# Who makes the low rows' one-hots of the input products of steps 0 and 1: ScalarE in place of GpSimd

## What is computed

```
def cell(h, x):                              # 64 steps, in order
    gi = x @ W_ih + b_ih
    gh = h @ W_hh + b_hh
    r = sigmoid(i_r + h_r); z = sigmoid(i_z + h_z)
    n = tanh(i_n + r * h_n)
    return (1 - z) * n + z * h
...
qx, sx, sc = _reorder_quantize_x(xf, up_reorder_index)
g = _qlinear(qx, sx, sc, w_gate, ...); u = _qlinear(qx, sx, sc, w_up, ...)
y = _qlinear(quantised(silu(g) * u), w_down, ...)
return x + y
```

## Time and profile before

| what | value |
|---|---|
| median of 3 runs | 2875.44 us (2875.31 to 2877.52) |
| the profiled execution, first to last instruction | 2879.2 us |
| TensorE matmuls busy | 2562.9 us (89%) |
| GpSimd busy | 1262.3 us (44%) |
| ScalarE busy | 1140.6 us (40%) |
| VectorE busy | 1685.2 us (59%) |

### The profile page before, as it was taken

The page is one execution under the profiler, slowest core; times in us unless marked ns, Lnnn a source line. Parts: engine busy times, 40 slices in busy tenths (PEclk is TensorE's granted clock), DMA queues, the critical chain, the costliest instruction groups (busy, mean ns, idle before and its releaser), DMA issues. The chain is left out here.

```text
span 2879.2 us, 154632 instructions
## 1 busy us (share of the span) xinstructions
PE 2562.9 (89%) x67605; PEld 1681.0 (58%) x67605; DVE 1685.2 (59%) x3398; ACT 1140.6 (40%) x2317; POOL 1262.3 (44%) x598
## 2 busy tenths in 40 slices
PE   2088999998889999999999999999996999999995
PEld 1066777776768888887675564655642444444442
DVE  8852222225632222225646778867592888888887
ACT  1321222225632222224702333323232777777773
POOL 0255666662046666664061363622700333333334
PEclk8599999999999999999999999999998999999998
DMA  6833222224422222226554253442432223232322
GB/s 193 239 85 77 74 73 71 73 71 112 131 63 71 74 73 70 73 71 167 152 135 127 92 151 118 115 156 85 129 143 93 74 84 95 84 95 84 95 63 53
DMA packets 234843, 293.74 MB, mean 102 GB/s; under 512 B 69581, under 2 KB 194023, under 8 KB 233895
## 3 DMA queue, kind: packets, MB, share of 16 engines
q1 hardware_dynamic: 212743, 240.84, 30.6%
q10 hardware_dynamic: 18304, 36.19, 3.6%
q0 software_dynamic: 3680, 15.21, 1.9%
HBM read 231.61 MB, written 60.45 MB: 101 GB/s over the span
## 5 line engine op out<-in xcount | busy, mean ns | idle before, releaser
L1145 PE MATMUL psum<-second_shared 64*32 64x384 f16 x32768 | 1026.0, 324 | 50.2 <-issue 31.3
L1153 PE MATMUL psum<-low_w,low_hot 64*32 64x384 f16 x16384 | 756.5, 324 | 2.0 <-issue 2.0
L1372 DVE TENSOR_SCALAR second_shared<-psum 32x384 f16<-32x384 f32 x496 | 272.3, 549 | 749.1 <-PE psum L1145 741.9
L953 POOL TENSOR_TENSOR low_hot<-first_shared,sum_mask 128x1024 f16<-128x1024 f16 x256 | 499.8, 1952 | 430.1 <-DVE first_shared L1359 183.8
L1145 PEld LDWEIGHTS psum<-second_shared 64*32 64x32 f16 x32768 | 561.5, 93 | 198.0 <-issue 89.8
L947 POOL TENSOR_TENSOR second_shared<-first_shared,whole_mask 128x2048 f16<-128x2048 f16 x128 | 462.5, 3614 | 460.1 <-PE psum L1145 348.2
L1044 ACT ACTIVATE second_shared<-psum 32x384 f16<-32x384 f32 x496 | 239.8, 483 | 801.9 <-PE psum L1145 795.9
L1233 PE MATMUL psum<-low_w,low_hot 64*64 64x384 f16 x12288 | 513.7, 326 | 19.9 <-issue 13.5
L1233 PEld LDWEIGHTS psum<-low_w,low_hot 64*64 64x64 f16 x12288 | 378.3, 108 | 150.4 <-issue 18.4
L310 PE MATMUL psum<-w_x,x_cols 128*64 128x512 f32 (+1 forms) x1856 | 312.0, 495 | 9.5 <-ACT x_cols L280 9.5
L1153 PEld LDWEIGHTS psum<-low_w,low_hot 64*32 64x32 f16 x16384 | 282.5, 93 | 56.8 <-issue 3.1
(11 more groups left out here) (286 smaller groups left out, 2746.6 us busy)
## 6 DMA issues: line engine op xcount, KB each, us to landing
low_w<-w_rows SPq DMA_DIRECT2D x384, 144.0 KB
low_w<-w_rows SPq DMA_DIRECT2D x256, 120.0 KB
second_shared<-w_rows SPq DMA_DIRECT2D x1024, 24.0 KB, 1.9
x_gates<-x_out ACTq DMA_DIRECT2D x58, 384.0 KB, 2.3
xg<-x_gates SPq DMA_DIRECT2D x58, 384.0 KB, 3.2
low_w<-w_rows SPq DMA_DIRECT2D x256, 72.0 KB
low_w<-w_rows SPq DMA_DIRECT2D x384, 48.0 KB
w_rows<-quantised SPq DMA_DIRECT2D x24, 384.0 KB, 4.9
```

The costliest lines, as they stand in the source:

```text
L953: nc.gpsimd.tensor_tensor(low_hot[:, buf].rearrange("p (s k) b -> p s k b", s=SUBS), low_a[:, slot, bass.ds(c, 1), :, :].rearrange("p a s ...
L1145: last = nc.tensor.matmul(run[m][u][j * Q:(j + 1) * Q, :], whole_hot[rows[u], m, sign, kk, j % 2 * Q:(j % 2 + 1) * Q], whole_w[rows[u], m, ...
L1153: nc.tensor.matmul(run[m][u][j * Q:(j + 1) * Q, :], low_hot[rows[u], m, kk, j % 2 * Q:(j % 2 + 1) * Q], low_w[rows[u], m, at:at + UC], sta ...
L1372: last = nc.vector.tensor_scalar(whole_w[u * B:u * B + Q, m, 0, bq, :], run[m][u][bq * Q:(bq + 1) * Q, :], 1.0 / HIGH_ONE, None, ALU.mult)
```

## The change

In steps 0 and 1 the `low_hot` tiles of m = 0 (the input product) are made by ACT, with the eight activations that `x_one_hots` uses, now in a function of its own, `low_hots`. GpSimd keeps every `whole_hot`, and `low_hot` of m = 1. On ACT the tile of block (0, 0) comes ahead of the clearing of the bases, and that of (c, 0) between the bases of (c, 0) and (c, 1). Since `hot_ok` of such a block no longer implies its `whole_hot`, TensorE waits for `whole_ok` too at blocks of m = 0.

```
--- before.py
+++ after.py
@@ -739,6 +739,10 @@
 
                     return 2 * NBK * t + 2 * c + m
 
+                def shared_hots(t, m):
+
+                    return t < FINE and m == 0
+
                 def x_slot(t):
 
                     return max(0, t - 1)
@@ -941,7 +945,8 @@
                             if m == 1 and t > 0:
                                 pool.wait_ge(placed, placed_by(t) + placed_for(t, c))
                                 pool.wait_ge(placed_second, placed_by(t) + placed_for(t, c))
-                            pool.wait_ge(hot_ok, block_no(t, m, c) + 1)
+                            if not fine:
+                                pool.wait_ge(hot_ok, block_no(t, m, c) + 1)
                             pool.wait_ge(run_ok[1], emptied(t, m, c))
                             if fine:
                                 nc.gpsimd.tensor_tensor(
@@ -949,7 +954,10 @@
                                     whole_a[:, m, bass.ds(c, 1), :].to_broadcast([P, 2 * BK, B]),
                                     whole_mask[:].rearrange("p s k -> p (s k)").unsqueeze(2).to_broadcast([P, 2 * BK, B]),
                                     ALU.mult).then_inc(whole_ok, 1)
+                                if shared_hots(t, m):
+                                    return
                                 pool.wait_ge(whole_ok, fine_no(t, m, c) + 1)
+                                pool.wait_ge(hot_ok, block_no(t, m, c) + 1)
                             nc.gpsimd.tensor_tensor(
                                 low_hot[:, buf].rearrange("p (s k) b -> p s k b", s=SUBS),
                                 low_a[:, slot, bass.ds(c, 1), :, :].rearrange("p a s b -> p (a s) b").unsqueeze(2).to_broadcast([P, SUBS, SK, B]),
@@ -1035,6 +1043,16 @@
                                         last = nc.scalar.activation(low_a[part * B:(part + 1) * B, ROWS_H, group::PB, 0, :], picked(n, slice(0, B)), ACT.Copy)
                                 last.then_inc(placed, 1)
 
+                        def low_hots(t, c, buf, slot):
+
+                            a.wait_ge(hot_ok, block_no(t, 0, c) + 1)
+                            a.wait_ge(run_ok[1], emptied(t, 0, c))
+                            for k in range(SK):
+                                last = nc.scalar.activation(low_hot[:, buf, k::SK, :],
+                                                            low_a[:, slot, bass.ds(c, 1), :, :].rearrange("p a s b -> p (a s) b"),
+                                                            ACT.Copy, scale=sum_scale[:, k:k + 1])
+                            last.then_inc(hot_ok, 1)
+
                         def bases(t):
                             def base(c, m):
 
@@ -1045,6 +1063,13 @@
                                                                     run[m][u][(2 + bq) * Q:(3 + bq) * Q, :], ACT.Copy, scale=1.0 / HIGH_ONE)
                                     last.then_inc(base_a[u], 1)
 
+                            def base_and_hots(c, m):
+                                base(c, m)
+                                if shared_hots(t, m):
+                                    low_hots(t, c, m, ROWS_X0)
+
+                            a.wait_ge(rows_of_in[ROWS_X0], FINE_ROWS_IN * (t + 1))
+                            low_hots(t, 0, 0, ROWS_X0)
                             for m in range(2):
                                 a.wait_ge(run_ok[1], emptied(t, m, 0))
                                 for u in range(2):
@@ -1052,18 +1077,11 @@
                                     for bq in range(2):
                                         last = nc.scalar.activation(whole_w[own, m, 1, bq, :], zero_row[own, :], ACT.Copy)
                                     last.then_inc(base_a[u], 1)
-                            pair_blocks(a, base, 1)
+                            pair_blocks(a, base_and_hots, 1)
 
                         def x_one_hots(t):
                             def make(c, buf):
-
-                                a.wait_ge(hot_ok, block_no(t, 0, c) + 1)
-                                a.wait_ge(run_ok[1], emptied(t, 0, c))
-                                for k in range(SK):
-                                    last = nc.scalar.activation(low_hot[:, buf, k::SK, :],
-                                                                low_a[:, ROWS_X2, bass.ds(c, 1), :, :].rearrange("p a s b -> p (a s) b"),
-                                                                ACT.Copy, scale=sum_scale[:, k:k + 1])
-                                last.then_inc(hot_ok, 1)
+                                low_hots(t, c, buf, ROWS_X2)
 
                             a.wait_ge(rows_of_in[ROWS_X2], LOW_ROWS_IN * (t - FINE + 1))
                             sum_blocks(a, make)
@@ -1170,8 +1188,12 @@
                                     w_ready = c * LOADED + (loaded_before(stage_of(t, m), m) + LOADED)
                                     whole_ready = c * WHOLE_LOADED + (t * NBK + 1) * WHOLE_LOADED
                                     hot_ready = c * 2 + (block_no(t, m, 0) + 2)
+                                    shared = c * 2 + (fine_no(t, m, 0) + 1)
                                     for value in (based, w_ready, whole_ready, hot_ready):
                                         pe.compute_val(value)
+                                    if shared_hots(t, m):
+                                        pe.wait_ge(whole_ok, fine_no(t, m, 0) + 1)
+                                        pe.wait_ge(whole_ok, shared)
                                     for u in range(2):
                                         pe.wait_ge(base_v[u], fine_no(t, m, 0) + 1)
                                         pe.wait_ge(base_v[u], based)
```

## The result

The changed kernel takes 2886.58 us (median of 5 runs, 2884.9 to 2888.23), and the kernel before, timed beside it, 2876.62 us: a ratio of 1.0036, with a 95% interval of 1.0023 to 1.0049, that is 6.6 to 14.1 us slower. The prediction was 2883.4 us, slower by 0.28%. One run of a later kernel, 3502 us at a granted clock of 0.74 instead of 0.96, is left out of every figure.

The account below looks back on a forecast made before the run. TensorE was taken as the bound, with GpSimd free a third of the time. Wait 6.2, step 1's start 2.6 - 1.45, clock 0.6: +7.95 us on 2875.4, giving 2883.4 us; its own range 2881 to 2887, overall 2878 to 2888.

Parts of the forecast that it names:

- the wait at the loop's head: TensorE at each loop head in steps 0 and 1: one more wait instruction, 0.10 us each, +6.2 us (3.1 to 8.1).
- No loss in the loop from ACT, no gain from GpSimd: Loop of steps 0 and 1: ACT keeps 3.3 us spare per block, GpSimd was already 2.0 us early; both worth 0.
- The rival in which ACT falls behind: ACT's tile takes twice as long, 4.9 us, and only step 1's start pays: 2887.8 us; 1 in 10.
- The nearly free wait: Loop head: the fifth wait costs its 51 ns or is hidden: 2877 to 2880 us; 2 in 10.
- The start of step 1: Before step 1's first matmul: ACT's tile delays the clears, +2.6 us; shorter cut, -1.45; slower clock afterwards, +0.6.
- its 1.45: Ahead of step 1: DVE's second cutting instruction no longer meets GpSimd's tile, shortening the chain up to `place` by 1.45 us.
- The clock term: Start of step 1: a longer TensorE pause prolongs the half clock, costing 0 to 1.3 us, taken as +0.6.
- The forecast's upper bound: Clock at step 1's start: half clock lasts at most 5.2 us, read from the start of step 0 after its 8.6 us pause.
- The start of step 0: Start of step 0: cost 0, since TensorE is released by the DMA of `whole_w` at 148.82 us.
- The rival "faster": Step 0: late weights land 7.5 us earlier and their pause goes, giving 2873.3 us; 0.5 in 10.
- a sign of being wrong: Step 0: the forecast would be wrong if TensorE's 7.5 us pause for a DMA of weights moved.
- the 0.69 for slower: Whole kernel: chance of being over 0.2% slower, from all of the ACT case and nine tenths of the forecast.

Follow-up runs that it names:

- before, again: The kernel before, unaltered, run and profiled a second time: ratio 1.0002.
- ScalarE waits (both): Changed kernel, but ScalarE (ACT) waits for `whole_ok` before each of its tiles and TensorE's extra wait goes: 2878.2 us, ratio 1.0008; repeated, 2875.66 us, 1.0.
- early tile: Changed kernel with ScalarE waiting for `whole_ok` instead of TensorE, and the tile of (0, 0) made ahead of `place`: 2875.64 us, ratio 0.9996.
- the wait alone: Kernel before plus only TensorE's extra wait at m = 0, GpSimd still making every tile: 2884.45 us, ratio 1.003; again, 2884.64 us, 1.0026.
- changed again: The changed kernel, unaltered, run and profiled a second time: 2883.78 us, ratio 1.0034.
- ten more waits: Kernel before plus ten TensorE waits at the loop's head on a constant long reached: 2908.68 us, ratio 1.011.
- fewer waits (all three): Redundant TensorE waits removed: from the kernel before, 2862.72 us; from the changed kernel, 2866.47 us; from the early-tile kernel, 2861.42 us.

## Why the prediction was right

**The direction came from the step named for it: the wait at the loop's head.** A pass of the loop over c, from one first matmul to the next, has nearly the same length in all later passes. Two heads in a row of step 1, before:

```profile
1205.14 0.36 PE L1145 MATMUL psum<-second_shared 64*32 64x384 f16 x8 [0.44 <-issue]
...
1221.51 0.36 PE L1145 MATMUL psum<-second_shared 64*32 64x384 f16 x8 [0.44 <-issue]
```

The same after the change, 16.42 us apart instead of 16.37:

```profile
1214.25 0.36 PE L1163 MATMUL psum<-second_shared 64*32 64x384 f16 x8 [0.52 <-issue]
...
1230.67 0.35 PE L1163 MATMUL psum<-second_shared 64*32 64x384 f16 x8 [0.52 <-issue]
```

Mean of the passes 9 to 31, in us:

| kernel | wait instructions at head, in body | step 0 | step 1 |
|---|---|---|---|
| before, again; ScalarE waits (both); early tile | 4, 4 | 16.339 or 16.340 | 16.369 |
| changed; the wait alone again | 5, 4 | 16.460 | 16.422 or 16.423 |
| changed again; the wait alone | 5, 4 | 16.410 | 16.422 |
| ten more waits | 9, 4 | 16.878 | 16.895 |
| fewer waits (all three) | 3, 3 | 16.104 to 16.108 | 16.137 or 16.138 |

Five more instructions cost 0.53 to 0.54 us a pass, 0.106 each, the spacing that the forecast took. One fewer at each of the two borders gives back 0.23. The single one of the change cost less: 0.07 or 0.12 in step 0 and 0.054 in step 1, 31 x (0.071 + 0.054) = 3.9 to 31 x (0.121 + 0.054) = 5.4 us against the 6.2 forecast and inside its bounds. In step 1 the head's step itself grew by 0.084, but other steps of the pass became shorter by 0.03. So the direction and the place were right, and the price of a single instruction was taken too high.

**No loss in the loop from ACT, no gain from GpSimd: right.** TensorE names neither; ACT has 3.46 us to spare, forecast 3.3. The rival in which ACT falls behind is out. The nearly free wait is out by its total (2877 to 2880 us), less clearly by its price: in step 1 the single instruction costs 0.054 us a pass, close to the 0.051 that this rival took.

**The start of step 1 was sized too high as well: +1.75 us forecast (2.6 - 1.45 + 0.6), 0.9 by the parts that repeat in every profile.** The tile cost 2.35, not 2.6: it began 0.02 us behind `place` instead of 0.16, and the clears followed 2.35 us later, so that TensorE started 4.7 us behind the end of `place` instead of the 5 expected. The cut gave back its 1.45: with the tile on GpSimd (six profiles) its second instruction takes 1742 to 1747 ns, without (seven) 293 to 295. The Trainium skill's rule on the port that VectorE and GpSimd share, where the second to issue is held until the first is done (SBUF — State Buffer, Who interferes with whom), agrees. From the cut's start to the first matmul the six profiles show 20.97 to 21.94 us, the five in which ScalarE makes the tile behind `place` 21.90 to 22.25: a mean difference of 0.55, less than 0.9 since the picks happened to be 0.3 us shorter in the second group. In the kernel before alone, from the first pick to the end of `place`, they took 13.51 us in one execution and 12.88 in the other.

**The clock term cost 0 in this pair, not 0.6, and stays open beyond it.** The half clock lasted 2.6 us in both. But in five of the eight profiles in which TensorE's pause ahead of step 1 was the short one (2.4 to 2.7 us), there was no half clock behind it. The kernel before again is among them:

```profile
802.67:805.27 2.60, 2.60 (x129) 2.10 (x137) 0.00 (x1) 1.43 (x4) 0.00 (x0) 1.00 0.02 6
```

There 129 matmuls ran in the first 2.6 us instead of 72, while in all five profiles with the long pause (4.8 to 5.0 us) it ran at half clock first. So the longer pause may cost something on the average, by an estimate from these rows up to 57 x 0.02 = 1.1 us (eight matmuls follow each other in 0.16 us); no run settles it. The forecast's upper bound was misread: ahead of step 0 the clock was at 0.50 not through the pause of 8.6 us, it had stood there long before (0.50 in 60:140).

**The start of step 0: right**, 148.24 us against 148.82, in profiles that lie between 147.7 and 149.7.

**The rival "faster" and the range.** The pause of step 0 did not go; from start to start it was 7.82 us before and 8.80 after. The prediction took a move of this pause for a sign of being wrong; since it was 6.60 in the second profile of the unchanged kernel, it could not serve as one. The first profile of the changed kernel had both pauses long, 1.0 and 3.0 us more than before's. With 3.75 + 1.67 for the wait and 0.2 net at step 1's start (21.90 - 21.67) that is its 9.5 us but for some tenths. The second profile had 9.0 and 7.7. Two of the forecast's chances don't follow from its own shares: within 0.2% they make 0.29, not 0.27, and faster 0.025, not 0.04; the 0.69 for slower is right.

**What stays open, and what was luck.** The traces place 4.5 to 6 us (wait 3.9 to 5.4, start about 0.6). From its first matmul to its last, step 0 takes 541.0 to 542.9 us in the four profiles with the wait and 537.0 to 539.4 in the five with four instructions, step 1 530.3 to 531.2 and 527.1 to 528.8: 6.0 us in both steps together on the average, 1.0 of it in the pause of step 0. The timed runs lost 9.96 and 7.2 us, the wait alone 7.2 and 8.0, with lower ends of the intervals at 4.9 to 6.6. By the medians a surplus of 1 to 4 us is left; it comes with TensorE's wait, not with the tiles, and its cause is not shown. The forecast's 7.95 came so near because terms taken too high stood where this surplus is, and that is luck; the direction and the step that causes it are not. In the four profiles with the wait the pause of step 0 was 8.5 to 9.0 us, in the five with four instructions 6.6 to 8.5. This may be a part of it, but the pause does not follow the count of instructions (8.3 with nine, 7.2 to 8.9 with three), and single profiles can't settle it.

## What to carry to other kernels

Where the bound engine runs a loop, count the wait instructions ahead of its first instruction, here two waits in each: at a head where TensorE stood idle, each one more cost 0.05 to 0.12 us on every pass, though its condition had long been true. Moving work between two engines with time to spare was worth nothing here, and the synchronisation that it needed cost nothing that shows on the engine with time to spare. Waits that follow from others are worth removing: here three of nine were 0.46% of the kernel.

## What the runs showed that was not expected

- Inside the body, where four wait instructions cost 0.12 us in all, one fewer took nearly all of it away: the last of the steps at that border fell from 0.24 to 0.13 us.
- With five instructions at the head the later passes lock to one length: step 0 runs at 16.410 or 16.460 us a pass, and the same kernel was seen at either. One more instruction thus costs 0.05 to 0.12 us, five more 0.53.
- A pause for late weights varied from 5.4 to 9.1 us between two executions of the unchanged kernel, and from 7.7 to 12.1 between two of the changed one.
